# TensorE reads its expert numbers sixteen tiles at a time instead of one per tile

## The reference, cut to what matters

```python
def _L0_ffn_ref(hidden_states, gate_w, sgate_w, w13, w2, shared_gate_up_w, shared_down_w):
    shared = _silu_and_mul(x @ shared_gate_up_w.T) @ shared_down_w.T
    shared = shared * jax.nn.sigmoid(x @ sgate_w.T)
    routing_weights = jax.nn.softmax((x @ gate_w.T).astype(jnp.float32), axis=-1)
    topk_w, topk_ids = jax.lax.top_k(routing_weights, TOP_K)
    def body(acc, ew):
        w13_e, w2_e, e = ew
        coef = jnp.sum(jnp.where(topk_ids == e, topk_w, 0.0), axis=-1)
        h = _silu_and_mul(x @ w13_e.T)
        return acc + (h @ w2_e.T) * coef[:, None], None

x = x + 0.5 * ffn(_layernorm(x))
x = x + attention(_layernorm(x))
x = x + 0.5 * ffn(_layernorm(x))
```

## Time and profile before

| | |
|---|---|
| median of 3 runs | 709.12 us (703.31 to 709.79) |
| the profiled execution | 704.64 us, its span 702.9 us |
| PE busy | 577.8 us, 82% of the span |
| DVE busy | 496.1 us, 71% |
| ACT busy | 413.4 us, 59% |
| POOL busy | 241.8 us, 34% |
| mean granted TensorE clock | 0.936 |

### The profile page before, as it was taken

How to read it: one execution, slowest core, us unless ns; L and a number is a source line. 1 busy time by engine, 2 the same in 40 slices (tenths; PEclk the granted TensorE clock), 3 DMA queues, 4 the chain that set the end, 5 groups by cost and what they waited for, 6 DMA issues and landing times.

```text
span 702.9 us, 14497 instructions
## 1 busy us (share of the span) xinstructions
PE 577.8 (82%) x4310; PEld 297.5 (42%) x4310; DVE 496.1 (71%) x1414; ACT 413.4 (59%) x830; POOL 241.8 (34%) x197
## 2 busy tenths in 40 slices
PE   4896578888870788999989999999989968889880
PEld 2453346555540344333322223333355645656550
DVE  6698866755555768888898888887476646666563
ACT  6477466655440567675837776768773335656540
POOL 3477136778762100000000000000027736766662
PEclk9999599999995699999999999999989989999995
DMA  5399946765765011101000000000004545777667
GB/s 174 126 305 346 303 128 116 124 113 94 117 88 135 0 35 35 35 1 35 1 2 1 1 1 1 1 1 1 1 1 151 188 135 90 123 124 124 114 94 201
DMA packets 56234, 64.37 MB, mean 92 GB/s; under 512 B 5729, under 2 KB 50273, under 8 KB 56162
## 3 DMA queue, kind: packets, MB, share of 16 engines
q0 software_dynamic: 16608, 21.77, 18.8%
q1 hardware_dynamic: 33040, 31.60, 14.9%
q10 hardware_dynamic: 6514, 10.10, 4.7%
HBM read 31.05 MB, written 32.39 MB: 90 GB/s over the span
## 4 chain that ended last, share of the span: by engine, by line
PE 43%; DMA 23%; DVE 10%; issue 9%; POOL 6%; ACT 5%; SPq 1%; ACTq 0%; POOLq 0%; DVEq 0%
DMA acc_dram<-R 15%; PE psum L1530 10%; PE psum L1500 9%; PE psum L1288 8%; POOL xg_dram L681 5%; PE psum L1513 5%; DMA R<-xg_dram 3%; PE psum L1496 3%; DVE m_part L1239 2%; PE psum L1517 2%; DVE W_ex L1046 2%; DMA acc_dram<-R,vals 1%; DMA R<-acc_dram 1%; DMA kT<-w_dram 1%; ACT W_ex L723 1%
## 5 line engine op out<-in xcount | busy, mean ns | idle before, releaser
L1239 DVE TENSOR_REDUCE m_part<-psum 128x1 f32<-128x512 f32 (+3 forms) x304 | 182.5, 657 | 30.8 <-PE psum L1500 29.2
L868 ACT ACTIVATE R<-psum 128x1024 f32<-128x1024 f32 x144 | 141.0, 1022 | 43.3 <-PE psum L1513 33.1
L692 POOL DMA_INDIRECT acc_dram<-R x88 | 138.1, 1569 | 66.7 <-DMA acc_dram<-R 29.1
L1288 PE MATMUL psum<-W_ex,R 128*128 x564 | 104.0, 322 | 2.3 <-ACT R L782 2.3
L708 POOL TENSOR_TENSOR R<-R 128x256 f16<-128x256 f32 x6 | 4.0, 693 | 280.3 <-ACT R L850 280.3
L1500 PE MATMUL psum<-kT,qTs 128*128 128x512 f16 (+3 forms) x384 | 98.7, 331 | 1.9 <-DVE m_part L1239 1.2
L681 POOL DMA_INDIRECT xg_dram<-R,o_tok x64 | 71.0, 1109 | 46.9 <-DVE o_tok L1007 28.0
L1530 PE MATMUL psum<-R,vals 128*32 128x512 f32 x576 | 76.7, 604 | 0.4 <-ACT oT L876 0.2
L782 ACT ACTIVATE R<-psum 128x512 f16<-128x512 f16 x94 | 55.6, 594 | 36.2 <-PE psum L1336 33.8
L1077 DVE SCALAR_TENSOR_TENSOR R<-psum,R 128x176 f32<-128x176 f32 x94 | 32.1, 341 | 57.2 <-ACT R L789 57.1
L1288 PE MATMUL psum<-xT,W_sh 128*128 128x512 f16 x264 | 64.1, 395 | 6.0 <-DVE R L1057 3.1
(11 more groups left out here) (190 smaller groups left out, 953.2 us busy)
## 6 DMA issues: line engine op xcount, KB each, us to landing
R<-xg_dram SPq DMA_DIRECT2D x88, 144.0 KB, 2.4
kT<-w_dram ACTq DMA_DIRECT2D x15, 512.0 KB, 5.9
xg_dram<-pad_sb SPq DMA_DIRECT2D x33, 144.0 KB
R<-acc_dram SPq DMA_DIRECT2D x16, 256.0 KB, 4.5
acc_dram<-rot_b SPq DMA_DIRECT2D x2, 1152.0 KB, 9.0
acc_dram<-ex SPq DMA_DIRECT2D x4, 576.0 KB, 3.4
kT<-w_dram SPq DMA_DIRECT2D x4, 384.0 KB, 4.2
acc_dram<-R POOLq DMA_INDIRECT x88
```

Of the source, the lines that this page charges most:

```text
L692: nc.gpsimd.indirect_dma_start(acc_dram[f][n % 2], bass.IndirectOffsetOnAxis(ap=tile_rows(n, I32)[:, D + NE:D + NE + 1], axis=0), y_sb[:, ...
L868: nc.scalar.activation(prob[:, n % 2, 2 * pair:2 * pair + 2, :].rearrange("p g n -> p (g n)"), psum[:, 1024 * pair:1024 * (pair + 1)], ACT ...
L1239: nc.vector.tensor_reduce(m_part[:, h:h + heads, kt // 4], ps, axis=AX.X, op=ALU.max).then_inc(free_of(e), 1)
L1288: ins = nc.tensor.matmul(o, stat(a, k), mov(b, k), start=first and n == 0, stop=last and n == 3 * k_parts - 1, **kw)
```

## The change

In the loop of `ffn`, the expert number is no longer read in every round for the next tile. In rounds -1, 15 and 31, at the same place in the round, TensorE reads the numbers of the next sixteen tiles (fifteen in the last group) into sixteen registers. The number of reads, 94 in the whole program, and every other instruction stay as they were.

```diff
-                    if s + 1 < NX:
-                        expert[s + 1] = pe.value_load(tab_e[0:1, s + 1:s + 2], min_val=0, max_val=NE - 1)
+                    if (s + 1) % 16 == 0:
+                        for i in range(s + 1, min(s + 1 + 16, NX)):
+                            expert[i] = pe.value_load(tab_e[0:1, i:i + 1], min_val=0, max_val=NE - 1)
```

## The result

| | before | after |
|---|---|---|
| median | 707.86 us (4 runs, 703.31 to 709.79) | 758.26 us (4 runs, 757.42 to 759.43) |
| span of the profiled execution | 702.9 us | 755.9 us |
| PE busy | 577.8 us | 572.6 us |
| mean granted TensorE clock | 0.936 | 0.908 |

The changed kernel is slower: 50.4 us between the medians, a ratio of 1.0732 with a 95% interval of 1.0697 to 1.0767. Executions of every kernel fall into a faster and a slower group: all ratios compare the faster ones alone, the medians are over all of them, and the traces of the run without the reads, of the one with the earlier read, of the stop at round 31 and of the two kernels timed on one chip are of slower ones.

A forecast was written before the change was run, and what follows sets the result against it. Additions at 2.25 to 2.3 us a tile and the loop through eight tile places bound the expert tiles. Stops and clock, +46.3 us, less 5 of gain, give +41 on 704.64: 746, taken as 747 us; range 724 to 763.

The forecast's parts named there:

- the gain term: Expert tiles of both `ffn`: shorter TensorE rounds bring additions from 2.36 to about 2.29 us a tile, 5 us off.
- the start of `ffn(0)`: Round -1 of `ffn(0)`: nothing covers the group of reads, first expert product 7.6 us late, +8 us.
- The price of a read: Each read in a group on TensorE's sequencer takes 0.64 us with its gaps, bounds 0.47 and 0.80.
- The rival that reads of a group overlap: Groups of reads: the next starts before the last finishes, a group costs 3.0 us; 706 us, no change; 5%.
- The stops in the tiles: Rounds 15 of both `ffn` and 31 of `ffn(1)`: +9.2, +9.6 and +8.5 us, each with 0.8 for the clock.
- the small covers: Parts of two stops expected to be hidden: about 0.4 us in `ffn(0)` round 15, 0.5 in `ffn(1)` round 31.
- Round 31 of `ffn(0)`: POOL's clearing of buffers covers 5.2 of the stop's 9.0 us: +3.8 us, and 0.8 for the clock.
- The start of `ffn(1)`: Round -1 of `ffn(1)`: reads partly lie under TensorE's 4.89 us idle wait for tile 3's load, +4 us.
- The clock: After each of four stops inside the tiles, a stretch at clock 0.50 delays about 0.8 us, +3.2 us.
- the buffers cover: Rival: token and result places carry the engines over some 9 us of a stop; 712 us, no change; 4%.
- TensorE's round was not the pace: Expert tiles; denies the rival that TensorE's round set the pace and 25.5 us come back: 725 us; 7%.
- reads of 0.80 us: Rival: all reads slower (+14 us) and 2 us a stop for the clock (+5): 766 us; 6%.

## Why the prediction was right

The direction, the main mechanism and the range held: 747 us forecast, 758.26 measured, inside 724 to 763. The size was low. The sum was +41 us on the profiled execution; between the medians it is +50.4, and between the two traces, which the sum was made for, 53.0. Of the 11.7 us that are missing 8.5 belong to the gain term, 2.6 to the start of `ffn(0)` and 1.5 to round 31 there, with 0.9 the other way in the rest; 2.3 of the 8.5 are the clock's, whose share was counted in the steps of the stops. That the result still lies in the range is in part luck: the room above the forecast was for dearer reads everywhere, and only those at the start of `ffn(0)` were dearer.

- **The price of a read, 0.64 us**: right. Starts lie 0.65 to 0.68 us apart in the groups inside the tiles. The rival that reads of a group overlap, for which I took the Trainium skill's remark on amortizing a `tensor_load` to speak ("DMA: Bandwidth & Descriptors", "Latency and other measured facts"), did not happen; reads in a row cost each its whole time. The floor of about 600 ns given there fits the spacing of whole reads and not the load instruction alone, which takes 0.30 us here.
- **The stops in the tiles**: right in sum. Predicted with their clock 10.0, 10.4 and 9.3 us, seen in the steps 10.0, 9.7 and 9.4. One stop alone gave 10.4. But the steps hold only the reads: the clock's share came one step later, and the small covers taken off for `ffn(0)` round 15 and `ffn(1)` round 31 do not show.
- **Round 31 of `ffn(0)`**: predicted 4.6, seen 6.1 us. The cover is real (the stop alone cost 4.8 of its 9.7 us). In the changed kernel the reads start at 187.7 us and tile 28's addition at 189.59, 1.9 us later; before, the read of this round started 3.0 us ahead of that addition, and in the run with this stop alone 3.4 us. The stop begins later against POOL's clearing, so less of it is covered.
- **The start of `ffn(0)`**: predicted 8, seen 10.6 us. I had seen one read of 1.48 us and allowed little for others; six of the sixteen took 0.7 to 1.0 us.
- **The start of `ffn(1)`**: predicted 4, seen 3.7 us.
- **The gain of 5 us**: this is the term that failed. It came from "the difference between 2.36 and about 2.29 us over some 40 tiles", with the belief that shorter rounds of TensorE would bring the additions down to their own period. Seen instead: 2.37 us a tile before and after in the 42 steps of `ffn(1)` away from the stops, and no gain without any reads either. Shorter rounds of TensorE only make it wait longer for tokens, 28.8 in place of 19.2 us. Why the pace stays at 2.37 and not at the 2.22 to 2.3 that successive additions can reach is open.
- **The clock**: 3.2 us predicted for four stops. The four steps behind the stops are 2.3 us longer than in the kernel before, and 3.3 and 5.3 us longer than with matmuls in the stops. The size was right; the place was one step further on.

Of the other rivals, the buffers cover about 0.6 us of a stop in `ffn(1)`, not 9; TensorE's round was not the pace; and reads of 0.80 us stayed confined to the start of `ffn(0)`, with the clock at about 1 us a stop and not 2. Two roundings in the working: 11.3 us for five tiles are 2.26 a tile, and 747 us is 5.3% on the median.

## What to carry to other kernels

A short blocking piece of sequencer work in every round was free here, because TensorE's round with it (2.13 us) stayed under the pace of the additions (2.36 us). Gathered into one place, the same work stood on the path: in full where nothing finished was stored behind it, and to one half or two thirds where POOL had other work to do. Before batching, find out how much is stored between the engine that will stop and the one that sets the pace. Where that one is fed just in time, spread the work out. Laying it under a wait that is there anyway gained nothing here, since it cost nothing where it was.

## What I had not expected of the hardware

A read from SBUF into a TensorE register takes 0.30 us for the load itself in most cases (median of 94). At the start of the tiles of `ffn(0)`, with a DMA share of 0.72 between 82.7 and 96.8 us of the changed kernel, six of sixteen took 0.7 to 1.0 us, and single ones in other kernels up to 1.48 us; that the DMAs are the cause is not shown. The first of two reads in a row in each round took 0.49 us (median). Matmuls put between the reads kept the granted clock at 1.00 through a stop of 10 us and lengthened a group of reads by only 0.2 to 0.5 us in all.
